# One product for the high and low part of the peaks, and their sum on VectorE

## The chip, the cores and the metric

The kernel runs on one core of one Trainium2 chip. The metric is the device time of one execution in microseconds (us). Three runs of the kernel before gave a median of 8592.96 us (8581.37 to 8603.45).

## The reference, cut to what matters

The program is a network of two layers on a graph of 6250 nodes and 206,250 edges (100,000 in both directions and a loop at each node), sorted by their target. The change is in the first layer's graph attention:

```
h = (x @ W).reshape(n, 8, 32)
a1 = sum(h * attn_l, -1);  a2 = sum(h * attn_r, -1)
e = leaky_relu(a1[src] + a2[dst], 0.2)
seg_max = segment_max(e, dst)
ex = exp(e - seg_max[dst])
denom = segment_sum(ex, dst)
out = segment_sum(h[src] * (ex / denom[dst])[:, :, None], dst)
```

Eight heads, so for each edge eight scores, and for each node eight maxima over its edges. A maximum over segments can't be had from a product of matrices, a sum can; much of what follows serves to get the maxima across.

## The kernel before, in words

The kernel works in stages, one behind the other: an opening (normalisation, projections, a table `h_dram` with a row of 272 numbers per node), the dense mix, the attention loop, the experts, the relations of the second layer, and the experts again. Only the attention loop (`attend`) is changed; it takes the time from about 440 to 3813 us.

*Tiling.* The edges lie in groups of 1024 (`G` = 8 rows of 128 edges; 203 groups), the nodes in 49 blocks of 128. A step of the loop handles one pair of a group and a block that it touches: 252 pairs with padding, and a few steps to fill the pipeline. Steps are unrolled by four in the loop.

*The ring.* GpSimd gathers the rows of a group's sources by eight indirect DMAs (line 853) into one of seven slots of `ring`. SyncE (lines 822 to 838) stands between: it waits until a group has landed, raises `ready`, then waits until VectorE has made the messages (`messages`) of the last pair of the group four back, and raises `room`, which GpSimd waits for. SyncE does this in order.

*The pipeline over pairs.* In step t each engine works on several pairs at once:

- ScalarE: the exponents of pair t+1 (L1033), the scores `sta` of group t+5 out of the ring (L1039), and the transposed one-hot `hot_t` of pair t+3 (L1045, L1047).
- VectorE: takes the running maxima of pair t+3 from `psI` (`ends` and `peaks`, L1150, L1151, L1165), the attention arguments of pair t+1 (L1153, L1154, L1161, L1174, L1183), the maximum `red` over the rows of edges for pair t+2 (L1157, L1167, L1177, L1181), the one-hot `hot` of pair t+3 (L1187), the scan over segments for group t+4 (L1191), the sums into `xb` (L1127, L1132), and last the messages of pair t+1 (L1197, L1201). Between parts that use each other's results stands `v.drain()`, which waits until the engine's earlier instructions have ended.
- TensorE: the sums of messages by node (L1064, half a pair at the start and half at the end of its step), the nodes' numbers spread over partitions (L940), the nodes' maxima brought back to the edges (L1085), the peaks brought to the nodes (L1093), and two transposes (L1098, L1102).

*The peaks.* For each edge that is the last of its segment `peaks` holds the maximum of the segment, for the other edges 0. The value is kept in two bf16 parts, the high one (L1151) and the rest `ends - high` (L1165). For each of the 8 rows of edges TensorE multiplies the one-hot matrix with the high part (8 columns, one for each head) and then with the low one, accumulated into the same 8 columns of `psX`. VectorE takes the maximum over the 8 rows straight from `psX` (L1157).

*Order.* VectorE's step starts with a wait for `turned`, raised by TensorE's last transpose (L1102). Ahead of L1187 it waits for `summed` (TensorE's L1064), ahead of L1201 for `weights` (ScalarE's L1033). TensorE waits for `shifts` (raised by L1181) ahead of L1085 and for `marked` (raised by L1187) ahead of L1093. There is no planner: the order is that in which the lines stand.

Of the kernel before, what the change touches and what calls it, by code (L numbers as in the profile page):

```python
# [5 lines left out]
P = 128  # L6
G = 8
# [5 lines left out]
HEADS = 8  # L13
# [16 lines left out]
ALU = mybir.AluOpType  # L30
ACT = mybir.ActivationFunctionType
AX = mybir.AxisListType
F32 = mybir.dt.float32
I32 = mybir.dt.int32
BF16 = mybir.dt.bfloat16
# [838 lines left out]
def one_of(eng, table, t, most):  # L874
    return eng.value_load(table[0:1, ds(t, 1)], min_val=0, max_val=most)
# [13 lines left out]
def attention(nc, z, k, S):  # L889
# [3 lines left out]
    with ExitStack() as c:  # L893
        sem = c.enter_context(semaphores(nc, "ga_"))
        sb = lambda n, s, d=F32: c.enter_context(nc.sbuf_tensor("ga_" + n, s, d))
        attend(nc, z, k, S)
        rows = k.xb[:].rearrange("p (b f) -> p b f", f=XW)
        heads = rows[:, :, 0:HC1].rearrange("p b (h w) -> p b h w", w=HW)
# [38 lines left out]
def spread_nodes(pe, k, psB, g, half):  # L937


    return pe.matmul(psB[:, half * 512:(half + 1) * 512], k.pick[:, ds(g % 64, 1)].to_broadcast([P, P]),  # L940
                     k.node_rows[:, ds(g // 64 * GE + half * 512, 512)], start=True, stop=True)


def attend(nc, z, k, S):
# [11 lines left out]
    GH = G * HEADS  # L956
    with ExitStack() as c:
        sem = c.enter_context(semaphores(nc, "ga_"))
        sb = lambda n, s, d=F32: c.enter_context(nc.sbuf_tensor("ga_" + n, s, d))
# [6 lines left out]
        apart = sb("apart", [P, GE])  # L966
        here = sb("here", [P, z.NCH * P])
        ends = sb("ends", [P, G, HEADS])
        peaks = sb("peaks", [P, 2, G, HEADS], BF16)
        red = sb("red", [P, HEADS])  # L970
        both = sb("both", [P, 2, 2, G + 1, HEADS])
        own = sb("own", [P, HEADS])
# [9 lines left out]
        psX = c.enter_context(nc.psum_tensor("ga_psX", [P, 512], F32))  # L982
# [5 lines left out]
        shifts, args, weights, messages, summed = (  # L988
            sem(x) for x in ("shifts", "args", "weights", "messages", "summed"))
        psQ_v = psI[:, 2 * P:2 * P + GH].rearrange("p (j h) -> p j h", j=G)  # L990
        psX_v = psX[:, 0:GH].rearrange("p (j h) -> p j h", j=G)
        psL_v = psX[:, P:P + G * LW].rearrange("p (j h a) -> p j h a", j=G, a=PARTS)
        w = psW[:, 0:2 * (G + 1) * HEADS].rearrange("p (u j h) -> p u j h", u=2, j=G + 1)
        iota = psN[:, 0:P].unsqueeze(1).to_broadcast([P, G, P])
        with nc.Block() as block:
            @block.vector
            def _(v):

                rows = k.a12[:].rearrange("p (b a) -> p b a", a=A2)
                left = apart[:, 0:z.NB * HEADS].rearrange("p (b h) -> p b h", h=HEADS)  # L1000
                parts = split[:].rearrange("p (b h a) -> p b h a", h=HEADS, a=PARTS)
                v.tensor_scalar(rows[:, :, 0:HEADS], rows[:, :, HEADS:], 0.0, k.least[:, 0:1], ALU.mult, ALU.add)
                v.tensor_copy(parts[:, :, :, 2], rows[:, :, HEADS:])
                v.drain()
                v.tensor_copy(parts[:, :, :, 0], rows[:, :, 0:HEADS])
                v.tensor_tensor(left, rows[:, :, HEADS:], parts[:, :, :, 2], ALU.subtract)
                v.drain()
                v.tensor_tensor(parts[:, :, :, 1], rows[:, :, 0:HEADS], parts[:, :, :, 0], ALU.subtract)
                v.tensor_copy(parts[:, :, :, 3], left)
                v.drain()  # L1010
                v.tensor_tensor(parts[:, :, :, 4], left, parts[:, :, :, 3], ALU.subtract)
                v.tensor_scalar(here[:], k.pair_node[:], k.place[:, 0:1], -1.0, ALU.add, ALU.mult)
        numbers(nc, k, sem, psN)
        with nc.Block() as block:
# [41 lines left out]
            @block.tensor  # L1056
            def _(pe):
                pe.sem_inc(turned, BASE - 5)
                pe.sem_inc(summed, BASE)
                pe.sem_inc(spread, BASE - 4)  # L1060

                def sum_up(t, u, part):
                    for j in part:
                        o = pe.matmul(psS[:, u % 2, 0:MROW], hot[:, u, j, :], msg[:, u % 2, j, :],  # L1064
                                      start=j == 0, stop=j == G - 1)
                    return o

                def step(t, u, group, block_no):
                    early = isinstance(t, int)
                    now = t + BASE if early else pe.snap(t + BASE)  # L1070
                    n0, n2, n3, n4 = (not early or t + q >= 0 for q in (0, 2, 3, 4))
                    if n0:

                        pe.wait_ge(messages, now)
                        sum_up(t, u, range(0, G // 2))
                    if n3:

                        pe.wait_ge(spent, now)
                        spread_nodes(pe, k, psB, group(3), 0)
                        spread_nodes(pe, k, psB, group(3), 1).then_inc(spread, 1)  # L1080
                    if n2:

                        pe.wait_ge(shifts, now)
                        for j in range(G):
                            pe.matmul(psL_v[:, j, :, :], hot_t[:, u % 2, j * P:(j + 1) * P],  # L1085
                                      split[:, ds(block_no(2) * LW, LW)], start=True, stop=True)
                    if n3:

                        pe.wait_ge(marked, now)
                        for j in range(G):  # L1090
                            ones = hot[:, (u + 3) % U, j, :].bitcast(BF16).rearrange("p (n h) -> p n h", h=2)[:, :, 1]
                            for q in range(2):
                                pe.matmul(psX_v[:, j, :], ones, peaks[:, q, j, :], start=q == 0, stop=q == 1)  # L1093
                    if n4:

                        pe.wait_ge(scanned, now)
                        pe.sem_inc(pe_go, 1)
                        pe.transpose(psI[:, 2 * P:2 * P + GH], scan[:], k.ident[0:GH, 0:GH])  # L1098

                    pe.wait_ge(staged, now)  # L1100
                    pe.sem_inc(pe_go, 1)
                    pe.transpose(psI[0:GH, 0:P], sta[:].rearrange("p j h -> p (j h)"), k.ident[:]).then_inc(turned, 1)  # L1102
                    if n0:
                        sum_up(t, u, range(G // 2, G)).then_inc(summed, 1)
                for t in range(-5, U):
                    step(t, t % U, lambda d: one_of(pe, k.pair_group, max(t + d, 0), z.NGT - 1),
                         lambda d: one_of(pe, k.pair_block, max(t + d, 0), z.NB - 1))
                with pe.Fori(1, z.T // U) as i, ExitStack() as held:
                    groups = Ahead(pe, held, "pe_g", k.pair_group, 3, U, z.NGT - 1)
                    blocks = Ahead(pe, held, "pe_b", k.pair_block, 2, U, z.NB - 1)  # L1110
                    groups.load(i * U)
                    blocks.load(i * U)
                    for u in range(U):
                        step(i * U + u, u, lambda d: groups.at(u + d), lambda d: blocks.at(u + d))

            @block.vector
            def _(v):
# [16 lines left out]
                def step(t, u, group, block_no):  # L1134
                    early = isinstance(t, int)
                    now = t + BASE if early else v.snap(t + BASE)
                    n0, n1, n2, n3 = (not early or t + q >= 0 for q in (0, 1, 2, 3))
# [7 lines left out]
                        pieces = split[:, ds(block_no(2) * LW, LW)].rearrange("p (h a) -> p h a", a=PARTS)  # L1145

                    v.wait_ge(turned, now)
                    if n3:
                        lasts = k.last[:, ds(group(3) * G, G)].unsqueeze(2).to_broadcast([P, G, HEADS])
                        v.tensor_tensor(ends[:], psQ_v, lasts, ALU.mult)  # L1150
                        v.tensor_tensor(peaks[:, 0, :, :], psQ_v, lasts, ALU.mult)  # L1151
                    if n1:
                        v.tensor_reduce(theirs[:], psL_v[:, :, :, 2:], AX.X, ALU.add)  # L1153
                        v.tensor_reduce(both[:, s1, 1, 0:G, :], psL_v, AX.X, ALU.add)  # L1154
                        v.tensor_tensor(mine[:, 0:HEADS], halves[:, :, 0], halves[:, :, 1], ALU.add)
                    if n2:
                        v.tensor_reduce(red[:], psX_v.rearrange("p j h -> p h j"), AX.X, ALU.max)  # L1157
                    v.drain()

                    if n1:  # L1160
                        v.tensor_tensor(both[:, s1, 0, 0:G, :], ring[:, ds(slot(group(1)), G), HC1:HROW], theirs[:],  # L1161
                                        ALU.add)
                        v.tensor_tensor(both[:, s1, 1, G, :], mine[:, 0:HEADS], mine[:, HEADS:], ALU.add)
                    if n3:
                        v.tensor_tensor(peaks[:, 1, :, :], ends[:], peaks[:, 0, :, :], ALU.subtract)  # L1165
                    if n2:
                        v.scalar_tensor_tensor(own[:], red[:], k.least[:, 0:1], tops[:, 0:HEADS], ALU.add, ALU.max)  # L1167
                        v.tensor_tensor(both[:, s2, 0, G, :], tops[:, 0:HEADS], tops[:, HEADS:], ALU.add)
# [38 lines left out]
                for t in range(-4, U):  # L1207
                    step(t, t % U, lambda d: one_of(v, k.pair_group, max(t + d, 0), z.NGT - 1),
                         lambda d: one_of(v, k.pair_block, max(t + d, 0), z.NB - 1))
                with v.Fori(1, z.T // U) as i, ExitStack() as held:  # L1210
                    groups = Ahead(v, held, "dve_g", k.pair_group, 1, U + 3, z.NGT - 1)
                    blocks = Ahead(v, held, "dve_b", k.pair_block, -1, U + 3, z.NB - 1)
                    groups.load(i * U)
                    blocks.load(i * U)
                    for u in range(U):
                        step(i * U + u, u, lambda d: groups.at(u + d), lambda d: blocks.at(u + d))
# [1222 lines left out]
```

## Time and profile before

| | |
|---|---|
| median of three runs | 8592.96 us |
| lowest and highest | 8581.37, 8603.45 us |
| profiled execution, span | 8625.7 us |
| profiled execution, any other time | none on the page |
| TensorE matmul busy | 5291.5 us (61%) |
| VectorE busy | 4192.2 us (49%) |
| GpSimd busy | 3723.7 us (43%) |
| ScalarE busy | 1501.9 us (17%) |
| granted TensorE clock, mean | 0.791 of full speed |

These are shares of the whole span, over stages with different limits. What the change is worth has to be read from the attention loop alone. The name of a releaser in a wait is inferred; where it names a transfer that ended long ago, the code has to say what the instruction waits for. Ends of TensorE's instructions are modelled.

### The profile page before, as it was taken

What the parts mean: (1) busy time and instruction counts of PE and PEld (TensorE: products, weight loads), DVE (VectorE), ACT (ScalarE), POOL (GpSimd) and SP (SyncE); (2) the same over time, 40 slices, a digit from 0 to 9 for tenths busy, and PEclk for the clock granted to TensorE, in tenths of its full rate; (3) what the DMA queues carried; (4) which work ended last, traced back from release to release, by engine and by line L of the source; (5) the groups of instructions that cost most, each with busy time, mean ns of one, the idle gap of its engine ahead of it and who ended that gap; (6) DMA issues with size and microseconds to landing.
All of it is one profiled execution on the core that took longest, in us unless ns stands there. A gap on an engine that the chain in (4) does not pass through costs nothing. (4 is left out here: it accounts for less than half of the span.)

```text
span 8625.7 us, 102556 instructions
## 1 busy us (share of the span) xinstructions
PE 5291.5 (61%) x25352; PEld 3622.4 (42%) x25607; DVE 4192.2 (49%) x9436; ACT 1501.9 (17%) x2795; POOL 3723.7 (43%) x3885
## 2 busy tenths in 40 slices
PE   6844554555554555445985999456656666655485
PEld 5423333333333333334663444344445444543363
DVE  5345555555555555573247100356556565655533
ACT  2112221222221222223431333000000000000131
POOL 4354444444444444413124000556656665665224
PEclk8967777777777777776998999777877787877698
DMA  4422222222222222223232344322323322333134
GB/s 147 138 76 71 67 70 69 63 69 71 70 66 70 68 67 69 68 74 104 80 90 66 155 160 165 98 83 86 88 85 88 88 86 86 88 87 81 58 121 136
DMA packets 360152, 770.67 MB, mean 89 GB/s; under 512 B 91010, under 2 KB 225056, under 8 KB 346720
## 3 DMA queue, kind: packets, MB, share of 16 engines
q0 software_dynamic: 174720, 490.64, 20.3%
q1 hardware_dynamic: 178256, 272.40, 9.2%
q10 hardware_dynamic: 7056, 6.43, 0.2%
q14 instruction: 93, 0.76, 0.0%
q8 instruction: 27, 0.44, 0.0%
HBM read 575.54 MB, written 208.31 MB: 91 GB/s over the span
## 5 line engine op out<-in xcount | busy, mean ns | idle before, releaser
L853 POOL DMA_INDIRECT ga_ring<-h_dram,src_at x1624 | 1556.7, 959 | 1772.2 <-SPq L838 1288.2
L853 POOL DMA_INDIRECT rg_ring<-y_dram,src_at x1624 | 1548.0, 953 | 1693.0 <-POOLq L931 701.1
L1638 PE MATMUL rg_psS<-rg_ring,rg_hot_w 128*128 x4032 | 1189.7, 453 | 265.4 <-issue 259.9
L1064 PE MATMUL ga_psS<-ga_msg,ga_hot 128*128 128x280 f32 x4032 | 1280.9, 476 | 58.9 <-issue 38.3
L1638 PEld LDWEIGHTS rg_psS<-rg_ring,rg_hot_w 128*128 128x128 f32 x4032 | 899.3, 230 | 565.0 <-issue 412.4
L1064 PEld LDWEIGHTS ga_psS<-ga_msg,ga_hot 128*128 128x128 f32 x4032 | 912.9, 235 | 349.2 <-issue 62.6
L1085 PE MATMUL ga_psX<-ga_split,ga_hot_t 128*128 x2032 | 107.3, 189 | 1177.4 <-DVE ga_split L1181 865.9
L1447 PE MATMUL rr_psY<-rr_wr,rr_xt 128*128 128x512 f32 x1568 | 676.2, 594 | 2.5 <-DMA rr_xt<-x_dram 2.5
L1751 DVE TENSOR_SCALAR rg_hot_t<-rg_psB,pair_node,place 128x1024 bf16<-128x1024 f32 x255 | 341.3, 1338 | 649.2 <-PE rg_psB L940 615.7
L1150 DVE TENSOR_TENSOR ga_ends<-ga_psI,last 128x64 f32<-128x64 f32 x255 | 55.3, 217 | 1187.6 <-DMA xb<-x 1094.8
L1085 PEld LDWEIGHTS ga_psX<-ga_split,ga_hot_t 128*128 128x128 bf16 x2032 | 83.6, 102 | 1292.6 <-issue 1275.1
L1201 DVE SCALAR_TENSOR_TENSOR ga_msg<-ga_psW,ga_ring 128x2112 f32<-128x2112 f32 x253 | 592.1, 2340 | 2.1 <-issue 2.1
L1033 ACT ACTIVATE ga_psW<-ga_arg 128x72 f32<-128x72 f32 x253 | 59.3, 234 | 2360.1 <-DVE ga_arg L1183 1684.3
L1718 DVE TENSOR_TENSOR rg_picked<-rg_psL,rg_rel 128x384 f32<-128x384 f32 x253 | 139.9, 553 | 667.6 <-DMA x_dram<-rr_xt 448.9
L940 PE MATMUL rg_psB<-node_rows,pick 128*128 x385 | 150.5, 447 | 502.3 <-DVE rg_hot_t L1751 377.9
L1447 PEld LDWEIGHTS rr_psY<-rr_wr,rr_xt 128*128 128x128 f32 x1568 | 298.7, 191 | 378.1 <-issue 374.7
L2123 POOL DMA_INDIRECT f_back_y<-yg_dram,f_pos x196 | 188.2, 960 | 570.6 <-DMA yg_dram<-f_y 378.1
L1187 DVE SCALAR_TENSOR_TENSOR ga_hot<-ga_psN,pair_node,dstf 128x1024 f32<-128x1024 f32 x255 | 326.7, 1281 | 199.0 <-DMA mo_xt<-xt_dram 172.6
L2114 POOL DMA_INDIRECT xg_dram<-f_row,f_pos x196 | 192.8, 984 | 523.5 <-DVE f_row L2235 475.8
L1093 PE MATMUL ga_psX<-ga_peaks,ga_hot 128*128 128x8 bf16 x4080 | 146.0, 168 | 360.9 <-DVE ga_hot L1187 300.4
L2188 PE MATMUL f_psH<-f_w,f_xt 128*128 x896 | 344.2, 507 | 34.7 <-issue 22.8
L2205 PE MATMUL f_psO<-f_w,f_hidt 128*128 x1344 | 339.2, 389 | 14.9 <-issue 8.0
(336 smaller groups left out, 7927.2 us busy)
## 6 DMA issues: line engine op xcount, KB each, us to landing
y_dram<-rr_big SPq DMA_DIRECT2D x98, 1024.0 KB
f_x<-xg_dram SPq DMA_DIRECT2D x224, 128.0 KB
yg_dram<-f_y SPq DMA_DIRECT2D x224, 128.0 KB
ga_ring<-h_dram,src_at POOLq DMA_INDIRECT x1624
rg_ring<-y_dram,src_at POOLq DMA_INDIRECT x1624
xg_dram<-x SPq DMA_DIRECT2D x2, 6272.0 KB, 35.4
f_w<-L_ffn_W SPq DMA_DIRECT2D x16, 512.0 KB
h_dram<-op_row SPq DMA_DIRECT2D x49, 136.0 KB
```

The source lines that it names most:

```text
L853: p.indirect_dma_start(ring[:, (g % R) * G + j, :], None, table, bass.IndirectOffsetOnAxis(ap=rows[:, g * G + j:g * G + j + 1], axis=0)).t ...
L1064: o = pe.matmul(psS[:, u % 2, 0:MROW], hot[:, u, j, :], msg[:, u % 2, j, :], start=j == 0, stop=j == G - 1)
L1085: pe.matmul(psL_v[:, j, :, :], hot_t[:, u % 2, j * P:(j + 1) * P], split[:, ds(block_no(2) * LW, LW)], start=True, stop=True)
L1187: v.scalar_tensor_tensor(hot[:, (u + 3) % U, :, :], iota, k.pair_node[:, ds(t + 3, 1)], k.dstf[:, ds(group(3) * G, G)].unsqueeze(2).to_bro ...
L1201: v.scalar_tensor_tensor(msg[:, s1, :, 0:HC1].rearrange("p j (h w) -> p j h w", w=HW), w[:, s1, 0:G, :].unsqueeze(3).to_broadcast([P, G, H ...
L1447: t = pe.matmul(psY[:, q % 2, :], xt[:, u, kc * P:(kc + 1) * P], wr[:, kc, q * 512:(q + 1) * 512], start=kc == 0, stop=kc == KC - 1)
L1638: o = pe.matmul(psS[:, u % 2, 0:C], hot_w[:, u % 2, j, :], rows[:, j, :], start=j == 0, stop=j == G - 1)
L1751: v.tensor_scalar(hot_t[:, (u + 3) % 2, :], psB[:], k.pair_node[:, ds(t + 3, 1)], k.place[:, 0:1], ALU.subtract, ALU.is_equal).then_inc(sp ...
L2114: p.indirect_dma_start(k.xg_dram[b >= half], bass.IndirectOffsetOnAxis(ap=plan.pos[:, q, b:b + 1], axis=0), row[:, u, :], None).then_inc(s ...
L2123: p.indirect_dma_start(back_y[:, u, q, :], None, k.yg_dram[h], bass.IndirectOffsetOnAxis(ap=plan.pos[:, q, b:b + 1], axis=0)).then_inc(y_i ...
L2188: t = pe.matmul(psH[:, u % 2, 0:HID], xt[:, u % 2, kc * P:(kc + 1) * P], w1[:, ds((e * KC + kc) * HID, HID)], start=kc == 0, stop=kc == KC ...
L2205: t = pe.matmul(psO[:, u % 2, 0:C], hidt[:, u % 2, q * P:(q + 1) * P], w2[:, ds((e * HC + q) * C, C)], start=q == 0, stop=q == HC - 1)
```

## The change

The two parts of the peaks lie side by side for each row of edges, so that one product with 16 columns makes both, into 16 columns of `psX`; nothing is accumulated there any more. VectorE adds the two halves at the head of its step into `whole`, and takes the maximum over the rows from `whole`, after a drain, with a second drain behind it. Nothing else moves.

```
-        peaks = sb("peaks", [P, 2, G, HEADS], BF16)
+        peaks = sb("peaks", [P, G, 2, HEADS], BF16)
+        whole = sb("whole", [P, G, HEADS])
...
-        psX_v = psX[:, 0:GH].rearrange("p (j h) -> p j h", j=G)
+        psX_v = psX[:, 0:2 * GH].rearrange("p (j q h) -> p j q h", j=G, q=2)
...
-                            for q in range(2):
-                                pe.matmul(psX_v[:, j, :], ones, peaks[:, q, j, :], start=q == 0, stop=q == 1)
+                            pe.matmul(psX_v[:, j, :, :], ones, peaks[:, j, :, :], start=True, stop=True)
...
                     v.wait_ge(turned, now)
+                    if n2:
+                        v.tensor_reduce(whole[:], psX_v.rearrange("p j q h -> p j h q"), AX.X, ALU.add)
                     if n3:
                         lasts = k.last[:, ds(group(3) * G, G)].unsqueeze(2).to_broadcast([P, G, HEADS])
                         v.tensor_tensor(ends[:], psQ_v, lasts, ALU.mult)
-                        v.tensor_tensor(peaks[:, 0, :, :], psQ_v, lasts, ALU.mult)
+                        v.tensor_tensor(peaks[:, :, 0, :], psQ_v, lasts, ALU.mult)
                     if n1:
                         v.tensor_reduce(theirs[:], psL_v[:, :, :, 2:], AX.X, ALU.add)
                         v.tensor_reduce(both[:, s1, 1, 0:G, :], psL_v, AX.X, ALU.add)
                         v.tensor_tensor(mine[:, 0:HEADS], halves[:, :, 0], halves[:, :, 1], ALU.add)
+                    v.drain()
                     if n2:
-                        v.tensor_reduce(red[:], psX_v.rearrange("p j h -> p h j"), AX.X, ALU.max)
-                    v.drain()
+                        v.tensor_reduce(red[:], whole[:].rearrange("p j h -> p h j"), AX.X, ALU.max)
+                        v.drain()
...
-                        v.tensor_tensor(peaks[:, 1, :, :], ends[:], peaks[:, 0, :, :], ALU.subtract)
+                        v.tensor_tensor(peaks[:, :, 1, :], ends[:], peaks[:, :, 0, :], ALU.subtract)
```

## Rows read from the trace of the kernel before

**Rows 1.** The page, its first line: span and number of instructions.
```profile
span 8625.7 us, 102556 instructions
```

**Rows 2.** Stretches: us, busy of PE, PEld, DVE, ACT, POOL, clock, DMA share, GB/s.
```profile
440.00:3740.90 3300.90, 1659.84 (x10656) 1170.07 (x10779) 1779.42 (x5135) 685.86 (x984) 1543.88 (x1611) 0.73 0.26 69
3740.90:3813.40 72.50, 54.52 (x380) 38.88 (x385) 64.68 (x189) 24.70 (x36) 0.00 (x0) 0.87 0.06 6
```

**Rows 3.** Waits in the loop: who waited for whom, us, times, longest.
```profile
POOL ga_ring L853 <- SPq L838: 1288.2, 108, 20.0
...
SPq L838 <- DVE ga_msg L1201: 2533.6, 129, 33.6
...
DVE ga_ends L1150 <- DMA xb<-x: 1094.8, 97, 30.0
DVE ga_hot L1187 <- DMA mo_xt<-xt_dram: 172.6, 40, 8.6
```

**Rows 4.** Timeline of one cycle: start, us, instruction, [idle before <-releaser].
```profile
3006.60 0.96 POOL L853 DMA_INDIRECT ga_ring<-h_dram,src_at  x1 [0.30 <-issue]
3007.04 0.22 DVE L1150 TENSOR_TENSOR ga_ends<-ga_psI,last 128x64 f32<-128x64 f32 x1 [12.39 <-DMA xb<-x]
...
3021.15 2.34 DVE L1201 SCALAR_TENSOR_TENSOR ga_msg<-ga_psW,ga_ring 128x2112 f32<-128x2112 f32 x1
...
3024.31 0.95 POOL L853 DMA_INDIRECT ga_ring<-h_dram,src_at  x1 [16.75 <-SPq L838]
...
3028.95 0.30 PE L1102 MATMUL ga_psI<-ident,ga_sta 128*64 128x128 f32 x1
3028.97 2.34 DVE L1201 SCALAR_TENSOR_TENSOR ga_msg<-ga_psW,ga_ring 128x2112 f32<-128x2112 f32 x1
...
3038.75 0.23 DVE L1150 TENSOR_TENSOR ga_ends<-ga_psI,last 128x64 f32<-128x64 f32 x1 [7.43 <-DMA xb<-x]
...
3043.25 0.95 POOL L853 DMA_INDIRECT ga_ring<-h_dram,src_at  x1 [0.30 <-issue]
3047.28 1.28 DVE L1187 SCALAR_TENSOR_TENSOR ga_hot<-ga_psN,pair_node,dstf 128x1024 f32<-128x1024 f32 x1 [4.94 <-DMA mo_xt<-xt_dram]
...
3052.51 0.95 POOL L853 DMA_INDIRECT ga_ring<-h_dram,src_at  x1 [8.30 <-SPq L838]
```

**Rows 5.** Timeline, TensorE's products with the peaks in one step.
```profile
3020.42 0.56 PE L1093 MATMUL ga_psX<-ga_peaks,ga_hot 128*128 128x8 bf16 x16 [0.88 <-DVE ga_hot L1187]
```

**Rows 6.** Timeline of VectorE, first part of one step.
```profile
3015.74 0.22 DVE L1150 TENSOR_TENSOR ga_ends<-ga_psI,last 128x64 f32<-128x64 f32 x1 [0.61 <-issue]
...
3016.01 0.35 DVE L1153 TENSOR_REDUCE ga_theirs<-ga_psX 128x64 f32<-128x192 f32 x1
3016.28 0.48 DVE L1154 TENSOR_REDUCE ga_both<-ga_psX 128x64 f32<-128x320 f32 x1
3016.68 0.16 DVE L1155 TENSOR_TENSOR a<-ga_split  x1
3016.75 0.22 DVE L1157 TENSOR_REDUCE ga_red<-ga_psX 128x8 f32<-128x64 f32 x1
3017.22 0.23 DVE L1161 TENSOR_TENSOR ga_both<-ga_ring,ga_theirs 128x64 f32<-128x64 f32 x1 [0.25 <-issue]
...
3017.79 0.42 DVE L1127 TENSOR_TENSOR xb<-xb,ga_psW 128x264 f32 x1
3018.29 0.31 DVE L1174 SCALAR_TENSOR_TENSOR ga_bent<-ga_both 128x144 f32<-128x144 f32 x1
```

**Rows 7.** Groups of VectorE's instructions in the loop: count, busy us, mean ns, idle before.
```profile
L1165 DVE TENSOR_TENSOR ga_peaks<-ga_ends,ga_peaks 128x64 bf16<-128x64 f32 x255 | 55.5, 218 | 0.1
...
L1151 DVE TENSOR_TENSOR ga_peaks<-ga_psI,last 128x64 bf16<-128x64 f32 x255 | 53.8, 211 | 0.0
```

**Rows 8.** Timeline of GpSimd, the first and the last wait for a slot.
```profile
512.38 0.95 POOL L853 DMA_INDIRECT ga_ring<-h_dram,src_at  x1 [18.68 <-SPq L838]
...
3731.04 0.95 POOL L853 DMA_INDIRECT ga_ring<-h_dram,src_at  x1 [8.43 <-SPq L838]
```

## The prediction

> **What bounds the kernel now.** I read the page first for the span, 8625.7 us [rows 1]. The change touches one stage only, the attention loop, so I asked for the busy time of its stretches. From 440 to 3740.9 us GpSimd gathers and no engine is busy for more than 54% (VectorE, 1779.4 of 3300.9 us). From 3740.9 to 3813.4 the gathers are over and VectorE is busy for 89% [rows 2]. At 21 VectorE instructions a step, the 189 of this last stretch are 9 steps, some 8 us each; the 253 steps of the loop at this pace would be some 2040 us, yet it takes 3370. So the loop is a cycle of waits and not an engine at its limit.
>
> The view of waits says who stands in the cycle [rows 3]. GpSimd waits 108 times, 1288.2 us in all, for SyncE's line 838 (a ring slot handed back), and SyncE there waits for VectorE's L1201, the messages that end a step. The other way round, VectorE waits 97 times at L1150, the head of a step (1094.8 us), and 40 times at L1187 (172.6 us). The name beside these two is a DMA that had long ended, so I took it that the real releaser is what the code waits for there: TensorE's transpose L1102, and the end of its sum L1064.
>
> The timeline shows the cycle once [rows 4]. GpSimd's last gather of a burst starts at 3006.60 and VectorE leaves its stall at 3007.04. Two steps follow without a gap, the second with its L1201 at 3021.15 for 2.34 us, and at 3024.31, 0.82 us after its end, the next burst of sixteen gathers starts. It lasts 19.9 us, to 3044.2. TensorE's L1102 is recorded at 3028.95, but VectorE gets past its head only at 3038.75; it goes on to its middle, and stops again at L1187 until 3047.28, 3 us after the last gather, though nothing is missing but TensorE's older work. Then half a step, and the next burst at 3052.51. So while gathers run, VectorE gets little done whatever it costs, and the path runs: burst, release about when its gathers end, the rest of a step or one or two whole steps, slot, burst. **A microsecond added to a step costs a microsecond only where the head of the step lies between a release and the next burst.**
>
> **The change part by part.**
> TensorE: line 1093 issues 16 products of 8 columns a step, now 8 of 16. The group takes 0.56 us, 0.17 of it the last product [rows 5], so a product comes each (0.56-0.17)/15 = 0.026 us; 8 fewer save 0.21 us. It stands between the mark (L1187) and the transposes, which VectorE needs at the next step's head; in the step ahead of the stall in [rows 4] L1102 ends at 3029.25 by its record and VectorE's messages at 3031.31, so TensorE is 2 us ahead. Where VectorE stalls, the release is tied to the burst. I take 0 of it; at most 0.21 us in the 97 stalled heads, -20 us.
>
> VectorE, head of the step: a reduction of 128 elements to 64, the sum of the two halves, is new, ahead of everything. In the step of [rows 6] the 192-element reduction is followed 0.27 us later, the 320-element one 0.40 us later, so 0.001 us an element, and 128 elements give 0.20 us.
> The maximum (L1157) moves behind the drain and gets a drain of its own. Before: L1155 starts at 3016.68, L1161 at 3017.22, 0.54 us with maximum and one drain. After: L1155's 0.16, a gap, 0.22 for the maximum, and the old gap of 0.25 to L1161. The new gap is between 0.08 (L1127's end at 3018.21 to L1174) and 0.25 (3016.97 to 3017.22). That is 0.71 to 0.88, so 0.17 to 0.34 more. L1161 takes a ring address from a register and L1174 none, like the maximum; so the low end is the nearest. Together 0.37 to 0.54; I take **0.40 us a step**. Nothing hides it: on VectorE each instruction waits for the one before, and everything behind (shifts, exponents, mark, messages) moves by as much. Bounds for what the trace doesn't show: 0.20 if the moved maximum costs nothing, 0.60 if both drains are slow ones.
> The maximum now reads SBUF in place of PSUM: 64 elements take 218 ns from SBUF (L1165) and 211 from PSUM (L1151) [rows 7], so no change. The Trainium skill ("VectorE: DVE Perf Modes", the section on the TRN2 errata) gives 58 cycles plus the elements for an SBUF source and 120 for a PSUM source; by that the moved maximum would be 0.06 us cheaper and the step 0.34 us longer, some 6 us less in all. The rows speak against it and I don't use it.
> The peaks (L1151, L1165) are written in pieces of 8 with a stride: same elements, 0. The wait at the head now stands before the sum: same semaphore, and the same instructions queue behind it. One drain more queues nothing but what is counted. No DMA moves, and SyncE and GpSimd issue what they did.
>
> How many steps pay: I followed GpSimd's waits over the whole loop in the timeline, from the first to the last of [rows 8]. 103 of them contain the end of a step. In 32 of them VectorE's last release is at L1187, with no head behind it: nothing is paid. In 11 such a half is followed by one whole step: 11 heads. In 31 there is one head, 31. In 29 there are two, 58. That is 100. The sums agree roughly: 1288.2 us of waits, less some 2 us each before VectorE is released and 0.8 us each from message to burst, leave some 1000 us, 124 steps of 8.06 us, of which the 43 halves behind L1187 (0.6 of a step each) take 26. With the 9 steps at the end it is **109 heads, 109 x 0.40 = 44 us**. The other 144 lie under bursts.
>
> Sum: profiled span 8625.7 + 44 = 8669.7 us. The page has no other time of that execution; its span stands 32.7 us over the median of the three runs, 8592.96 (8581.37 to 8603.45), so I put the 44 on the median: **8637 us**, +0.5%.
>
> **The rivals.**
> *Every step pays.* If releases don't depend on the burst but on VectorE's own previous step, through something that the records hide, all 253 heads count: 101 us, 8694. For it: the stalls begin right behind a step's end. Against it: they end with the burst, and without gathers there are none [rows 2]. The Trainium skill leans this way ("SBUF — State Buffer", the section on who interferes with whom: a DMA never contends with an engine, and TensorE never waits on anyone); the trace has TensorE's result 9.5 us late during a burst, so I go by the trace.
> *The cover is larger.* Steps between bursts could absorb the time: the head of a step runs while TensorE still finishes what L1187 waits for. Only the 9 last steps would then pay, 4 us: 8597, no change. For it: the 43 releases at L1187 do just that. Against: in most whole steps the rows show no idle time at L1187.
> *Faster, through TensorE.* L1102 is recorded 4.6 us after a burst's start and is held; a TensorE result before that point gets through. If 0.21 us less of products lets the transpose through before the hold, the head and middle of the next step (3.5 us from L1150 to L1187) are done under the burst in the 60 cycles where they now follow it: -210 us, and with half of the heads then hidden +20: 8403. It decides at the moment at which results are held, some 4 us behind a burst's start; against it, VectorE's own 0.40 us pushes the same transpose later than the products bring it forward.
> *The change does less than it says*: if the product of 16 columns costs as two of 8, TensorE is as before and the time the forecast's.
>
> **How the numbers follow.** Forecast 0.61, with 0.30 to 0.60 us by 100 to 115 heads: 8622 to 8662. Larger cover 0.21, every step 0.12, faster 0.06. I leave out the last two; the range for 8 in 10 is 8600 to 8685. A difference under 0.3% (26 us) can't be told from none here. Slower by more: 0.12 and all but 0.02 of 0.61, so 0.71. Within: 0.21 and that 0.02, so 0.23. Faster: 0.06.
>
> **What would show it.** L1093's successor has half the products and a group of some 0.35 us. From the first instruction of a step to the addition with the ring 1.87 us in place of 1.48. Steps in the last stretch 0.40 us longer. GpSimd's wait for slots up by some 40 us, and the waits at L1187 down by some us. TensorE's saving is nowhere. The forecast is wrong if the number of waits at L1150 or L1187 changes by more than ten, if a burst's distance to the next changes where no head lies between, or if the head grows by under 0.2 us.

## The result and the profile after

Before: 8588.34 us, median of 4 runs (8581.37 to 8603.45). After: 8519.17 us, median of 4 (8506.42 to 8537.74). The ratio is **0.9919 [0.9902, 0.9935]**: faster by 69 us, where 8637 us had been forecast, with 0.06 for any gain beyond 26 us. The profiled execution of after has a span of 8519.2 us, 106.5 less than [rows 1]. That is more than the 69 us between the medians, because before's profiled execution is some 37 us above its median and above all four of its timed runs, while after's lies at its median. So the two traces below show the kinds of change well, and their sums somewhat too large.

The page of after, its first rows: span, then busy time and instructions of each engine.
```profile
span 8519.2 us, 99238 instructions
...
PE 5332.2 (63%) x23566; PEld 3598.2 (42%) x23567; DVE 4273.6 (50%) x9690; ACT 1503.2 (18%) x2795; POOL 3722.5 (44%) x3885
```
The two stretches that answer to [rows 2], same columns:
```profile
440.00:3616.50 3176.50, 1654.85 (x8811) 1126.62 (x8811) 1855.19 (x5380) 687.23 (x984) 1542.16 (x1611) 0.75 0.27 72
3616.50:3690.00 73.50, 53.04 (x310) 36.33 (x310) 65.77 (x198) 24.15 (x36) 0.07 (x1) 0.88 0.06 6
```
The same 1611 GpSimd instructions are through after 3176.5 us in place of 3300.9: **124 us come out of the stretch with gathers**, although VectorE is busy 76 us longer in it. Behind the last gather after is some 18 us longer than before. The last steps explain 3 of them (the last messages end 76.2 us behind the start of the last gather, in place of 73.5), and the rest I did not follow.

The waits of after, which answer to [rows 3] (who waited for whom, us, times, longest):
```profile
POOL ga_ring L853 <- SPq L838: 1179.9, 163, 19.9
...
DVE ga_whole L1149 <- DMA xb<-x: 599.1, 95, 20.0
...
DVE ga_hot L1190 <- DMA mo_xt<-xt_dram: 477.9, 83, 9.7
```
L1149 is now the head of a step and L1190 what L1187 was. GpSimd waits 108 us less. Its count rises to 163 only through 62 waits of some 0.30 us, the pace of its own issue; those over 1 us number 101, and 103 before. **The wait at the head has halved, 1094.8 to 599.1 us, and the wait at the mark has grown from 40 times to 83 and from 172.6 to 477.9 us.** That is the result in two rows: VectorE is let through its head earlier, does head and middle while the gathers still run, and stops at the mark.

One cycle of after (timeline, in order of time), beside [rows 4]:
```profile
3019.07 0.95 POOL L853 DMA_INDIRECT ga_ring<-h_dram,src_at  x1 [7.30 <-SPq L838]
...
3023.82 0.36 PE L1093 MATMUL ga_psX<-ga_peaks,ga_hot 128*128 128x16 bf16 x8 [0.88 <-DVE ga_hot L1190]
...
3024.41 0.30 PE L1102 MATMUL ga_psI<-ident,ga_sta 128*64 128x128 f32 x1
3024.55 2.34 DVE L1204 SCALAR_TENSOR_TENSOR ga_msg<-ga_psW,ga_ring 128x2112 f32<-128x2112 f32 x1
...
3033.41 0.29 DVE L1149 TENSOR_REDUCE ga_whole<-ga_psX 128x64 f32<-128x128 f32 x1 [6.52 <-DMA xb<-x]
...
3034.77 0.27 DVE L1160 TENSOR_REDUCE ga_red<-ga_whole 128x8 f32<-128x64 f32 x1
3035.29 0.22 DVE L1164 TENSOR_TENSOR ga_both<-ga_ring,ga_theirs 128x64 f32<-128x64 f32 x1 [0.25 <-issue]
...
3038.00 0.95 POOL L853 DMA_INDIRECT ga_ring<-h_dram,src_at  x1 [0.31 <-issue]
3042.04 1.28 DVE L1190 SCALAR_TENSOR_TENSOR ga_hot<-ga_psN,pair_node,dstf 128x1024 f32<-128x1024 f32 x1 [4.81 <-DMA mo_xt<-xt_dram]
...
3044.11 2.34 DVE L1204 SCALAR_TENSOR_TENSOR ga_msg<-ga_psW,ga_ring 128x2112 f32<-128x2112 f32 x1
3046.38 0.27 DVE L1149 TENSOR_REDUCE ga_whole<-ga_psX 128x64 f32<-128x128 f32 x1
3048.24 0.23 DVE L1164 TENSOR_TENSOR ga_both<-ga_ring,ga_theirs 128x64 f32<-128x64 f32 x1 [0.26 <-issue]
...
3055.33 0.95 POOL L853 DMA_INDIRECT ga_ring<-h_dram,src_at  x1 [16.38 <-SPq L838]
```
The group of products takes 0.36 us in place of 0.56, and the head 1.88 (3033.41 to 3035.29) and 1.86 us: both as forecast. L1102 ends at 3024.71 by its record, and VectorE has its result 8.7 us later, still 4.6 us before the burst's last gather starts. The mark is held until 3042.04, 3.1 us after that gather's end, as it was before.

Beside the rows I counted two things over the whole loop. First, the mean distance from the start of one burst of sixteen gathers to the start of the next, for the cycles in which VectorE ends two messages between them and for those with three. Second, by the trace's semaphore events, how long behind L1102's recorded end its signal comes. I call a signal held when it is more than 1 us late:

| | held | median delay of the held, us | two messages, us (cycles) | three messages, us (cycles) | last gather starts, us |
|---|---|---|---|---|---|
| before | 102 | 14.7 | 28.9 (50 cycles) | 37.8 (40) | 3739.9 |
| after | 109 | 7.8 | 27.9 (46) | 35.9 (38) | 3615.6 |

Of the held, 5 before and 6 after have no event of their own in the trace; the next event stands in for it, which makes the counts slightly too high. Some 50 cycles at 1.0 us and 40 at 1.9 are 126 us, the 124 that came out. The sum's signal (for the mark) has a median delay of 15.7 us before and 15.1 after, and comes 2.9 and 2.7 us behind the burst.

### The profile page after: what moved, and what is told of

Read it like the earlier page. It is cut to its first block and busy times, and to the rows that moved or that the text cites. A ratio compares the mean times of both kernels' runs of the same rounds, so it can differ in the third digit from the quotient of the medians.

```text
span 8519.2 us, 99238 instructions
## 1 busy us (share of the span) xinstructions
PE 5332.2 (63%) x23566; PEld 3598.2 (42%) x23567; DVE 4273.6 (50%) x9690; ACT 1503.2 (18%) x2795; POOL 3722.5 (44%) x3885
## 5 line engine op out<-in xcount | busy, mean ns | idle before, releaser
L853 POOL DMA_INDIRECT ga_ring<-h_dram,src_at x1624 | 1555.3, 958 | 1649.6 <-SPq L838 1179.9
L1065 PE MATMUL ga_psS<-ga_msg,ga_hot 128*128 128x280 f32 x4032 | 1303.5, 481 | 123.6 <-issue 74.4
L1065 PEld LDWEIGHTS ga_psS<-ga_msg,ga_hot 128*128 128x128 f32 x4032 | 922.1, 237 | 432.8 <-issue 106.5
L1190 DVE SCALAR_TENSOR_TENSOR ga_hot<-ga_psN,pair_node,dstf 128x1024 f32<-128x1024 f32 x255 | 326.8, 1282 | 491.1 <-DMA mo_xt<-xt_dram 477.9
L1086 PE MATMUL ga_psX<-ga_split,ga_hot_t 128*128 x2032 | 106.5, 188 | 711.7 <-DVE ga_split L1184 446.9
L1093 PE MATMUL ga_psX<-ga_peaks,ga_hot 128*128 128x16 bf16 x2040 | 94.2, 174 | 672.9 <-DVE ga_hot L1190 599.7
L940 PE MATMUL rg_psB<-node_rows,pick 128*128 x512 | 181.4, 436 | 448.5 <-DVE rg_hot_t L1754 345.9
L2117 POOL DMA_INDIRECT xg_dram<-f_row,f_pos x196 | 193.1, 985 | 525.7 <-DVE f_row L2238 477.9
L1149 DVE TENSOR_REDUCE ga_whole<-ga_psX 128x64 f32<-128x128 f32 x254 | 71.7, 282 | 660.2 <-DMA xb<-x 599.1
L1046 ACT ACTIVATE ga_apart<-ga_psB,ga_here 128x1024 f32<-128x1024 f32 x255 | 281.6, 1104 | 590.1 <-DMA mo_xt<-xt_dram 578.9
L1093 PEld LDWEIGHTS ga_psX<-ga_peaks,ga_hot 128*128 128x128 bf16 x2040 | 70.9, 101 | 699.3 <-DVE ga_hot L1190 619.0
```

The costliest lines, as they stand in the source:

```text
L853: p.indirect_dma_start(ring[:, (g % R) * G + j, :], None, table, bass.IndirectOffsetOnAxis(ap=rows[:, g * G + j:g * G + j + 1], axis=0)).t ...
L1046: act.activation(apart[:], psB[:], ACT.Square, bias=here[:, ds(t + 3, 1)])
L1190: v.scalar_tensor_tensor(hot[:, (u + 3) % U, :, :], iota, k.pair_node[:, ds(t + 3, 1)], k.dstf[:, ds(group(3) * G, G)].unsqueeze(2).to_bro ...
L2117: p.indirect_dma_start(k.xg_dram[b >= half], bass.IndirectOffsetOnAxis(ap=plan.pos[:, q, b:b + 1], axis=0), row[:, u, :], None).then_inc(s ...
```

## The experiments

**Theory A**: while gathers run, each of TensorE's products that stands in front of the transpose puts its signal off; eight fewer bring it forward. **Rival B**: the gain is VectorE's new order of work. **Rival C**: the cost is not the product but its weights, which are loaded from a tile with a step of two. **Rival D**: what counts is the number of products in a step, wherever they stand.

Each kernel was timed in three rounds beside the one before, in three batches, each on its own chip; ratios are to before in the same batch. The kernel before was traced only in the first comparison, so where a trace of e1 to e7 is set beside before's, a difference between chips is in it too. The kernel before took 8685.11 us in the first (8642.69 to 8727.18), **6782.69 in the second** and 8599.25 (8574.66 to 8616.42) in the third. More on the second below.

**e1_sixteen.** After, with sixteen products again; VectorE's new order stays.
```
-pe.matmul(psX_v[:, j, :, :], ones, peaks[:, j, :, :], start=True, stop=True)
+for q in range(2):
+    pe.matmul(psX_v[:, j, q, :], ones, peaks[:, j, q, :], start=True, stop=True)
```


> The kernel after, but with sixteen products a step again: high and low part go into their own eight columns, so VectorE's work is that of after and TensorE's count that of before. Theory A (while gathers run, TensorE's signals come out late by some 0.6 to 0.9 us for each product that stands in front of them): the waits at the head of VectorE's step go back to about 1000 us, and the time to that of before plus VectorE's 0.4 us on about 100 heads, 8610 to 8640. Rival B (the gain comes from VectorE's side, from the new order of reads, waits and drains): as after, 8510 to 8530. Rival C (what costs is a weight load whose elements are read with a step of two): as under A, since the eight more loads have that step.

Measured 8793.76 us, 1.0125 [1.009, 1.0161]. With sixteen products again the change is a loss of 109 us, so B falls. The loss is larger than A had forecast (8610 to 8640 us, a ratio of 1.003 to 1.006): I had priced VectorE's part too low. Its waits:
```profile
POOL ga_ring L853 <- SPq L838: 1426.2, 165, 20.6
...
DVE ga_whole L1150 <- DMA xb<-x: 1216.4, 98, 29.5
...
DVE ga_hot L1191 <- DMA mo_xt<-xt_dram: 121.0, 31, 9.8
```
Head and mark have changed back, and further. One cycle of its timeline, from the last step before a stall to the next burst (the burst began at 1022.99; L1191 is the mark here and L1205 the messages):
```profile
1027.89 2.34 DVE L1205 SCALAR_TENSOR_TENSOR ga_msg<-ga_psW,ga_ring 128x2112 f32<-128x2112 f32 x1
...
1041.95 0.96 POOL L853 DMA_INDIRECT ga_ring<-h_dram,src_at  x1 [0.30 <-issue]
1046.00 0.29 DVE L1150 TENSOR_REDUCE ga_whole<-ga_psX 128x64 f32<-128x128 f32 x1 [15.77 <-DMA xb<-x]
...
1049.75 1.28 DVE L1191 SCALAR_TENSOR_TENSOR ga_hot<-ga_psN,pair_node,dstf 128x1024 f32<-128x1024 f32 x1
...
1063.02 0.96 POOL L853 DMA_INDIRECT ga_ring<-h_dram,src_at  x1 [20.11 <-SPq L838]
```
The release at the end of the burst, 3.1 us behind the last gather's end, now finds VectorE at its head: 3.75 us of head and middle, and no wait at L1191, lie behind it. In after's cycle the same release finds VectorE at the mark. The burst came 40.03 us after the one before, against 36.26 in after's.

**e2_high_only.** Before, with the second product of each row left out: the maxima lack the low part. VectorE's work is that of before.
```
-for q in range(2):
-    pe.matmul(psX_v[:, j, :], ones, peaks[:, q, j, :], start=q == 0, stop=q == 1)
+pe.matmul(psX_v[:, j, :], ones, peaks[:, 0, j, :], start=True, stop=True)
```


> The kernel before with the low part's products left out (eight products of eight columns; the maxima then lack their low part): VectorE as before, TensorE's count as after. Theory A and rival C: the hold goes as in after and VectorE's 0.4 us are not paid, 8470 to 8500, head waits near 600 us. Rival B: as before, 8580 to 8600.

Measured 8557.48 us, 0.9841 [0.9805, 0.9878]: **eight products fewer are worth 128 us** (106 to 169 by the interval) where VectorE is left alone. Its waits:
```profile
POOL ga_ring L853 <- SPq L838: 1170.1, 106, 23.9
...
DVE ga_hot L1186 <- DMA mo_xt<-xt_dram: 583.5, 87, 11.4
DVE ga_ends L1149 <- DMA xb<-x: 558.4, 88, 22.2
```
The wait has moved from the head (558.4 for 1094.8 us) to the mark (583.5 for 172.6), with VectorE's order unchanged. With e1 this shows the cause: the number of products moves the release of the head, and the time with it. It does not show why the products count.

**e3_contiguous.** After, with eight products more, unread, whose weights are read without a step.
```
 pe.matmul(psX_v[:, j, :, :], ones, peaks[:, j, :, :], start=True, stop=True)
+pe.matmul(psX[:, 448:456], hot[:, (u + 3) % U, j, :].bitcast(BF16)[:, 0:P],
+          k.ident[:].bitcast(BF16)[:, 0:8], start=True, stop=True)
```


> The kernel after with eight more products a step, at the place of the peaks' products, whose weights are read with a step of one and whose result nobody reads. Theory A: the count is what matters, so as the kernel with sixteen products, 8610 to 8640. Rival C: the step of two is what costs, so as after, 8515 to 8535.

Measured 8781.4 us, 1.0101 [1.0064, 1.0138], not to be told from e1, and like it above my 8610 to 8640. C falls: it is the product, whatever its weights. The head waits as in e1:
```profile
DVE ga_whole L1151 <- DMA xb<-x: 1226.3, 97, 15.9
```

**e4_late.** After, with eight such products behind the transpose and ahead of the second half of the sum.
```
+for j in range(G):
+    pe.matmul(psS[:, u % 2, 320:328], hot[:, u, j, :].bitcast(BF16)[:, 0:P],
+              k.ident[:].bitcast(BF16)[:, 0:8], start=False, stop=False)
```


> The kernel after with eight more products a step behind the last transpose, ahead of the second half of the sum, whose result nobody reads. Theory A in the form that only what stands in front of a signal delays it: the head waits stay near 600 us, and the end of the sum comes with the end of the burst anyway, so 8515 to 8550. Rival D (the whole number of products in a step counts, as the engine falls behind as a whole): as the kernel with sixteen products, 8600 and more.

Measured 8644.25 us, 0.9946 [0.9923, 0.997]. On the same chip e3, with its eight unread products ahead of the transpose, took 137 us more. So the place counts for most of it, as A has it. Its waits at head and mark:
```profile
DVE ga_whole L1152 <- DMA xb<-x: 705.4, 89, 20.8
...
DVE ga_hot L1193 <- DMA mo_xt<-xt_dram: 441.8, 73, 12.6
```
Whether D holds for a small part is not shown. The head waits some 106 us more than in after, and the transpose's median delay is 10.0 us against 7.8, but the traces are of two chips and the intervals of the ratios (0.9919 for after) overlap.

**c_after, e5_half_rows, e6_short, e7_twentyfour** ran on the second chip. There nothing is held: in all four traces L1102's signals come at most 0.014 us behind its recorded end. c_after is after, unchanged.

> The kernel after, as it is, beside the others on their chip. 0.992 of before, as it was first measured.

Measured 6827.32 us, 1.0066 [1.0049, 1.0082], where I had expected 0.992: **on this chip the change is a loss of 44.6 us.** Two steps of it:
```profile
1498.81 0.30 PE L1102 MATMUL ga_psI<-ident,ga_sta 128*64 128x128 f32 x1
...
1501.22 0.27 DVE L1149 TENSOR_REDUCE ga_whole<-ga_psX 128x64 f32<-128x128 f32 x1
...
1502.12 0.96 POOL L853 DMA_INDIRECT ga_ring<-h_dram,src_at  x1 [0.99 <-SPq L838]
...
1506.87 0.30 PE L1102 MATMUL ga_psI<-ident,ga_sta 128*64 128x128 f32 x1
1507.02 2.34 DVE L1204 SCALAR_TENSOR_TENSOR ga_msg<-ga_psW,ga_ring 128x2112 f32<-128x2112 f32 x1
...
1509.28 0.27 DVE L1149 TENSOR_REDUCE ga_whole<-ga_psX 128x64 f32<-128x128 f32 x1
```
VectorE does a step each 8.06 us without idling, gathers running all the while; 253 of them are 2039 us, and GpSimd's 203 groups of eight gathers at 1.26 us are 2046, so both stand at their limit. With a step of 7.65 us, which the last stretch of before shows, VectorE would need 1935 us, some 110 less than GpSimd. This fits a loss of 44.6 us and not of all 101 (253 steps at 0.40 us): most of the 0.40 us goes into what VectorE had to spare. It is an estimate, as the kernel before was not traced on this chip. Its waits, and then its group of gathers (count, busy us, mean ns, idle before):
```profile
POOL ga_ring L853 <- SPq L838: 48.1, 77, 5.5
...
DVE ga_whole L1149 <- issue: 31.1, 61, 0.6
...
DVE ga_whole L1149 <- PE ga_psI L1102: 23.2, 7, 6.2
```
```profile
L853 POOL DMA_INDIRECT ga_ring<-h_dram,src_at x1624 | 1558.3, 960 | 536.1 <-issue 487.9 <-SPq L838 48.1
```
The head waits 54 us here in all, where it waited 599.1 us for the name of a DMA alone.

**e7_twentyfour** is e1 with eight more products.
```
 for q in range(2):
     pe.matmul(psX_v[:, j, q, :], ones, peaks[:, j, q, :], start=True, stop=True)
+pe.matmul(psX[:, 448:456], ones, k.ident[:].bitcast(BF16)[:, 0:8], start=True, stop=True)
```


> The kernel with sixteen products and VectorE's work of after, and eight more products whose result nobody reads: 24 a step. Theory A, each product delays the signal by as much: the head waits can grow only up to the end of the burst, where nearly all of them were with sixteen, so the time saturates, 1.012 to 1.022 of before. If every product is paid in full (eight were worth some 170 us), 1.03 or more.

Measured 6831.14 us, 1.007 [1.0053, 1.0087]: sixteen products more than after change nothing that can be told from noise where nothing is held.

**e5_half_rows** is before with gathers of 544 in place of 1088 bytes a row (the other half of each ring row is a constant, and the table is read in rows half as long, so the values are not the graph's): do the gathers' bytes hold TensorE's signals?
```
-p.indirect_dma_start(ring[:, (g % R) * G + j, :], None, table,
+p.indirect_dma_start(ring[:, (g % R) * G + j, 0:hi], None,
+                     table.rearrange("n (a f) -> (n a) f", a=2),
...
-v.tensor_scalar(rden[:], heads[:, :, :, D], 1e-30, None, ALU.max)
+v.tensor_scalar(rden[:], heads[:, :, :, D], 1.0, None, ALU.max)
...
+v.memset(ring[:].rearrange("p r f -> p (r f)"), 0.5)
```


> The kernel before with the first half of each gathered row only (544 of 1088 bytes, as many transfers; ring values are then not those of the graph). Theory A with the gathers' bytes as what holds TensorE's signals: the hold is shorter, the waits at the head of the step fall well under 1000 us, and the time falls to 8450 to 8550. If not the bytes but the number of descriptors or their issue on GpSimd holds the signals, the waits stay within 10% and the time within 0.5% of before.

Measured 6798.93 us, 1.0024 [1.0014, 1.0034]. With nothing held it says nothing on the question.

**e6_short** is after with VectorE's cost cut: the moved maximum loses its own drain, and its two readers are put into the third part, behind a drain that stands there anyway.
```
 v.tensor_reduce(red[:], whole[:].rearrange("p j h -> p h j"), AX.X, ALU.max)
-v.drain()
...
-v.scalar_tensor_tensor(own[:], red[:], k.least[:, 0:1], tops[:, 0:HEADS], ALU.add, ALU.max)
...
-v.tensor_copy(pieces[:, :, 0], own[:])
+v.scalar_tensor_tensor(own[:], red[:], k.least[:, 0:1], tops[:, 0:HEADS], ALU.add, ALU.max)
+v.scalar_tensor_tensor(pieces[:, :, 0], red[:], k.least[:, 0:1], tops[:, 0:HEADS], ALU.add, ALU.max)
```


> The kernel after with no drain more than before: the maximum stands with the second part of the step, own and the high piece are both made from it in the third part (the cast goes), the low piece in the fourth. TensorE as after. The head of the step is then 1.68 us in place of 1.88. If VectorE's time between bursts is on the path, 0.2 us on 100 to 250 steps: 20 to 50 us faster than after, 0.986 to 0.990 of before. If it is covered, as after.

Measured 6782.68 us, 1.0000 [0.9991, 1.001]: 44.6 us less than after, within the 20 to 50 expected (the ratio of 0.986 to 0.990 took a gain from after for granted, which this chip does not give). The loss of c_after is gone, so it had been VectorE's time. GpSimd waits only 9.9 us for slots, 48.1 in c_after.

**The third batch** ran the same kernels where signals are held again.

c2_after, after unchanged:

> The kernel after once more, beside the others on their chip. Where the kernel before takes some 8600 us (TensorE's signals held while gathers run): 0.990 to 0.994 of it. Where it takes some 6783 us (no signal held): 1.006 to 1.007.

Measured 8525.43 us, 0.991 [0.9886, 0.9934]: the result again.

e6b_short:

> The kernel after with no drain more than before, as it was run where nothing is held (there 45 us faster than after and equal to before). Where signals are held, the 0.2 us a step are saved between bursts: 20 to 50 us faster than after, 0.984 to 0.989 of before. Under rival B, that VectorE's time is covered there, as after.

Measured 8498.58 us, 0.9893 [0.9871, 0.9916]. It is 27 us under after, within the 20 to 50 expected, though the intervals overlap; the ratio lies just outside my 0.984 to 0.989. **It is the best version**: faster than before where signals are held, and where they are not it costs nothing against before.

e5b_half_rows:

> The kernel before with half of each row gathered, as many transfers of half the bytes (values not those of the graph). Where signals are held: if the gathers' bytes hold them, head waits fall well under 1000 us and the time under 0.985 of before; if their number or their issue does, the waits stay within 10% and the time within 0.995 to 1.005. Where nothing is held, 1.002 as measured.

Measured 8591.39 us, 0.9996 [0.998, 1.0011]. Its waits:
```profile
POOL ga_ring L853 <- SPq L838: 1194.2, 106, 24.0
...
DVE ga_ends L1152 <- DMA xb<-x: 969.2, 97, 28.7
...
DVE ga_hot L1189 <- DMA mo_xt<-xt_dram: 208.3, 56, 9.3
```
Half the bytes leave 969.2 of 1094.8 us at the head, and no time is gained. So the bytes are not what holds the signals, at most a small part of it. The trace rules out one thing more: a gather's data now goes in half as many packets of 4352 bytes (25,984 in place of 51,968 over the loop). What stayed is the number of gathers, and GpSimd's work of issuing them.

e7b_twentyfour:

> Twenty-four products a step, VectorE as in after. Where signals are held: theory A with a delay for each product ends at the end of the burst, where sixteen already put it, so 1.010 to 1.022 of before; if each product is paid in full, 1.03 or more. Where nothing is held, 1.007 as measured.

Measured 8853.28 us, 1.0293 [1.027, 1.0316]. I had expected 1.010 to 1.022, on the argument that with sixteen products the signal comes at the end of the burst already and can't come later. It missed: e1 had not been at that end in all cycles. By the events, 67 of 99 held signals of the transpose come within 6 us behind the end of a burst in e1, and 91 of 104 here, though their median delay hardly grows (16.9 to 17.2 us). The four in a row, the first and last from the third batch, the others from the first:

| products ahead of the transpose | ratio | head's wait, us | two messages, us | three messages, us |
|---|---|---|---|---|
| 8 (c2_after) | 0.991 | 593.6 | 27.8 | 35.9 |
| 16 (e1) | 1.0125 | 1216.4 | 30.0 | 39.1 |
| 16, half of them unread (e3) | 1.0101 | 1226.3 | 30.1 | 39.3 |
| 24 (e7b) | 1.0293 | 1417.6 | 31.4 | 39.5 |

```profile
DVE ga_whole L1149 <- DMA xb<-x: 593.6, 93, 20.6
```
```profile
DVE ga_whole L1151 <- DMA xb<-x: 1417.6, 100, 48.8
```
The direction is the same from row to row. What the last eight products cost is less certain: from e1 to e7b the times differ by 60 us and the ratios by 1.7%, some 145 us, because the kernel before itself is 86 us slower on e1's chip.

## Why the prediction was wrong

**The step that failed** is TensorE's term: "Where VectorE stalls, the release is tied to the burst. I take 0 of it; at most 0.21 us in the 97 stalled heads, -20 us." I priced eight products at their recorded time, 0.21 us, which is right for the record (0.36 for 0.56 us) and says nothing of when the result can be used. Under a burst they put it off by some 7 us in the median (7.4 in e2 against 14.7 in before, on another chip), some 0.9 us each. By e2 that is worth 128 us, where I had allowed at most 20. The traces of before already held the sign: in [rows 4] the head was released at 3038.75, during the burst, and the mark at 3047.28, behind it. Two releases of one engine at two different points are not both tied to the burst's end. I wrote "release about when its gathers end" for both; in fact the distance of the first from the burst's end is what the change moves.

**VectorE's 0.40 us was right.** Head 1.86 to 1.88 us, and an unheld step 8.06 us in the last stretch (L1149 at 3634.80 and 3642.86) against 7.65 before (L1150 at 3758.77 and 3766.42). Its parts came out otherwise, though: the new sum holds the head for 0.20 us, as worked out; the moved maximum was not free, with 267 ns from SBUF for 213 from PSUM. The Trainium skill ("VectorE: DVE Perf Modes", the section on the TRN2 errata) would have made it cheaper. That does not show here: this reduction is dearer from SBUF, by 0.05 us, though it also stands at another place now, behind a drain.

**Its weight, 109 heads and 44 us, was too low.** e1, where VectorE's cost stands alone, loses 109 us (78 to 140 by its interval), and after against e2 some 0.8%, 67 us. The first is rather the price of the rival in which every step pays (101 us), but not its mechanism: the heads still wait under bursts. That the signal itself comes later with the longer head (median delay 16.9 us in e1, 14.7 before) would fit; as these are two chips it is not shown. My check of the count was also off: I had taken 8.06 us a step from 72.5 us for nine steps, where two heads of the last stretch lie 7.65 us apart, so that the 1000 us make 131 steps and not 124.

**The third rival had the right engine and side, and 8403 us with a wrong mechanism.** No transpose slipped through ahead of the hold: 109 signals are held in after, 102 before. The hold is shorter, and partly: head and middle are taken out of the path in a part of the cycles, by 1.0 and 1.9 us in the mean and not 3.5.

**Signs.** I had written that the forecast fails if the waits at head or mark change in number by more than ten: the mark's went from 40 to 83. GpSimd's wait for slots fell by 108 us and did not rise by 40. The group of products, the head and the last steps came as described.

**The two terms may not simply add.** e2's -128 and e1's +109 would leave -19, and -69 was measured. With VectorE's longer head eight products fewer seem to be worth more (1.0125 by e1 to 0.991 by c2_after, some 185 us). Each of the first two is uncertain by some 31 us to either side, and the chips differ, so this is not shown beyond doubt. On the chip without held signals VectorE's time alone is +44.6.

**Open.** What holds the signals: it comes with the bursts, counts TensorE's products and hardly the gathers' bytes. In e5b, with half the bytes, the transpose's median delay is 12.1 us (14.7 in before, on another chip), and no time is gained. The number of gathers, or the way by which TensorE's instructions reach it, would fit; neither was tried. Whether TensorE computes late behind its records, or only signals late, the trace can't tell. Nor was it tried whether executions that leave no records behave so; all times here are of ones that do. This is the rival that matters most, because the traces hint at it. A gather's landing leaves sixteen semaphore events, 25,984 over the loop's 1624 gathers. The four traces without held signals keep 25,512 to 25,841 of them, and the ten with held signals 4992 to 6161. So on the chips where TensorE's signals are late the recording itself loses most of these events. Whether the recording holds the signals, or both suffer from a third thing, no run here tells; if it is the first, an execution without records may show neither the hold nor this gain.

## What to carry to other kernels

Here a record's end was not when the result could be used. Compare each producer's record with its reader's start, and where they lie microseconds apart, price an instruction in front of that result by this distance and not by its busy time. If two waits for one engine are released at different points of a burst, the earlier one may be movable, as here, and the work between them is what can be won. Take a price that depends on such a hold from more than one chip: this change gave -0.8% and -0.9% on two and +0.7% on another, and its version with VectorE's cost removed gave -1.1% and 0.0% (e6b, e6).

## What the hardware showed beside it

**One kernel, two speeds by chip.** The kernel before took 8588, 8685 and 8599 us where signals were held and 6783 on the chip where none were, 21% less. With the same instructions, after's last gather of the attention loop starts at 3615.6 us in the one and at 2503.1 in the other: 1112 of the 1692 us between the spans (8519.2 and 6827.2). Of the other 580, 511 lie in the second loop with gathers, that of the relations (2555.8 us from the start of its first gather to the end of its last in the one, 2044.5 in the other); there GpSimd waits 533.7 us for slots in after, and in c_after not at all. In the attention loop the difference is the held signals, some 15 us in the median at the mark: GpSimd waits 1179.9 us for slots in the one and 48.1 in the other. TensorE's granted clock differs too, 0.75 in after's stretch with gathers and 0.90 in c_after's, but its busy time there only by 111 us (1654.85 and 1543.39), so slower products don't make the difference. Each chip had its runs at one time only, so that it is the chip and not the hour is not shown, and why one has no held signals stays open. The Trainium skill ("SBUF — State Buffer", the section on who interferes with whom) has TensorE wait on nobody and a DMA contend with no engine. It speaks of the ports to SBUF. c_after is as it says; in the runs of the other chips TensorE's results come late while gathers run, whatever the reason, and for the forecast the measurement decides.

**The name beside a wait.** Nearly all of the head's wait is put to a DMA that had long ended, in every run with held signals (1094.8 us in before, with 28.2 for the transpose's name). In c_after, where nothing is held, what is left of it carries the transpose's name (23.2 us, 7 times) or none.

**Products ahead of a held signal** cost some 0.9 to 1.1 us each in its median delay (7.4 to 14.7 by e2 and before; 7.8 to 16.9 by after and e1, each pair from two chips), with 0.026 us of recorded time. With nothing held, sixteen more of them cost 3.8 us in the whole kernel (6831.14 against 6827.32), within the intervals.
